# Spreading one much-gathered table row over 1024 copies, and moving a row norm's last step from VectorE to ScalarE, in a four-stage graph network kernel

## The reference, cut to what matters

```
net 0 (SAGE):  three layers  h = relu(h @ Ws + mean_over_edges(h[src]) @ Wn + b)
net 1 (GAT):   two attention layers with graph norms, then a mean over edges
net 2 (jumping knowledge), h = x, for i in 0..3:
    agg = segment_sum((h * norm_src)[src], dst) * norm_dst
    h = relu(agg @ Ws[i] + bs[i])
    h = relu(batchnorm(h) * gammas[i] + betas[i]);  xs.append(h)
  out = relu(max(xs) @ lin1_w + lin1_b)
net 3 (GCN):   three layers
```

## Time and profile before

| what | value |
|---|---|
| median of 3 runs | 6672.85 us (6664.08 to 6673.42) |
| the profiled execution, its own time | 6654.82 us |
| its span in the trace | 6653.0 us |
| mean granted TensorE clock | 0.814 |
| busy: PE, DVE, POOL, ACT | 71%, 68%, 61%, 46% of the span |
| DMA | 1292.14 MB, mean 194 GB/s |

### The profile page before, as it was taken

One profiled execution on the slowest core, in us unless ns is written; L12 is line 12 of the kernel. 1 busy time (PEld: TensorE's weight loads), 2 busy tenths in 40 slices (PEclk: granted clock), 3 DMA queues, 4 the chain that ended last, 5 costly groups with the idle time before them and its releaser, 6 DMA issues. The chain is left out here.

```text
span 6653.0 us, 86619 instructions
## 1 busy us (share of the span) xinstructions
PE 4751.0 (71%) x23528; PEld 3218.9 (48%) x23532; DVE 4503.1 (68%) x13695; ACT 3061.7 (46%) x6979; POOL 4040.8 (61%) x3991
## 2 busy tenths in 40 slices
PE   6999998989988724796335455545999996598221
PEld 4667776645568403694223233312666664465111
DVE  4788887333369827888885566776888885654554
ACT  3566665643334104454444444434888873364000
POOL 5566664754445477667667676675333335674777
PEclk9999998989999755795557766766999998799555
DMA  6999886987778424795445697855777776675232
GB/s 160 244 270 278 252 253 202 296 241 244 239 230 265 127 53 105 236 348 162 127 134 148 130 138 133 141 96 144 269 271 276 275 255 185 205 212 165 87 91 82
DMA packets 1104141, 1292.14 MB, mean 194 GB/s; under 512 B 133903, under 2 KB 815679, under 8 KB 1097390
## 3 DMA queue, kind: packets, MB, share of 16 engines
q1 hardware_dynamic: 973518, 1032.63, 49.1%
q0 software_dynamic: 130144, 253.97, 18.9%
HBM read 607.93 MB, written 682.10 MB: 194 GB/s over the span
## 5 line engine op out<-in xcount | busy, mean ns | idle before, releaser
L570 POOL DMA_INDIRECT jk_layer_msg<-jk,idx_jk x588 | 592.9, 1008 | 255.1 <-issue 175.3
L1057 PE MATMUL jk_layer_sum_ps<-ident,jk_layer_weighted 128*128 128x128 f32 x784 | 182.3, 375 | 540.3 <-ACT jk_layer_weighted L1023 540.3
L2084 POOL TENSOR_TENSOR rows_moved<-rows_x_in,w_lonely_row 128x512 f32<-128x512 f32 x98 | 152.3, 1554 | 563.0 <-DVE rows_x L671 537.0
L1057 PEld LDWEIGHTS jk_layer_sum_ps<-ident,jk_layer_weighted 128*128 128x128 f32 x784 | 116.4, 185 | 655.7 <-ACT jk_layer_weighted L1023 655.7
L696 PE MATMUL sage_nodes_h_ps<-sage_nodes_h_t,w_ws 128*128 128x512 f32 x784 | 353.7, 594 | 0.0
L1198 DVE COPY sage_h<-sage_turn 128x512 f32<-128x512 f32 x98 | 67.8, 692 | 421.0 <-PE sage_turn L687 421.0
L2283 PE MATMUL gcn_end_sum_ps<-ident,gcn_end_rows 128*128 128x128 f32 x196 | 54.7, 435 | 394.5 <-DVE gcn_end_rows L2276 394.5
L894 ACT ACTIVATE sage_nodes_h_t<-sage_nodes_h_ps,w_b_c 128x512 f32<-128x512 f32 x392 | 248.2, 684 | 172.6 <-PE sage_nodes_h_ps L696 172.2
L570 POOL DMA_INDIRECT sage_msg<-h,idx x196 | 185.8, 948 | 230.6 <-ACT sage_weighted L1023 151.6
L696 PE MATMUL jk_layer_h_ps<-jk_layer_sum_t,w_jk_w 128*128 128x512 f32 x392 | 315.0, 900 | 0.2
L1079 DVE TENSOR_TENSOR_SCAN jk_layer_sum_t<-goes_on,jk_layer_sum_t,jk_layer_sum_ps 128x512 f32<-128x512 uint8 x196 | 249.8, 1274 | 92.7 <-PE jk_layer_sum_ps L1057 92.7
(11 more groups left out here) (454 smaller groups left out, 16050.7 us busy)
## 6 DMA issues: line engine op xcount, KB each, us to landing
h<-sage_nodes_h SPq DMA_DIRECT2D x196, 512.0 KB
h_t<-sage_h_t SPq DMA_DIRECT2D x98, 512.0 KB, 4.9
h<-sage_h SPq DMA_DIRECT2D x98, 512.0 KB
jk_t<-jk_layer_h_t SPq DMA_DIRECT2D x196, 256.0 KB
rows_layers<-jk_t SPq DMA_DIRECT2D x49, 1024.0 KB, 6.0
r<-rows_h SPq DMA_DIRECT2D x98, 512.0 KB, 7.3
second_x_in<-u SPq DMA_DIRECT2D x147, 260.0 KB
jk<-jk_layer_h SPq DMA_DIRECT2D x147, 256.0 KB
```

Source lines behind the costliest of these rows:

```text
L570: pool.indirect_dma_start(out=into[:, g.number % depth, s, :], out_offset=None, in_=table, in_offset=bass.IndirectOffsetOnAxis(ap=index_ti ...
L1057: mm = pe.transpose(ps[:, c, at_s], self.weighted[:, g.b, s, c * P:(c + 1) * P], self.K.ident[:])
L2084: pool.tensor_tensor(moved[:, g.b], x_in[:, g.number % 3], to_subs(W.lonely_row), ALU.add).then_inc(lonely_added.sem, 1)
```

## The change

It has two parts that don't touch each other.

First, the row shared by lonely sources gets 1024 copies in each of jk0, jk1 and jk2 (rows SLOTS to SLOTS + 1023), and `K.idx_jk` of an edge with a lonely source is SLOTS plus the low ten bits of its place. The copies are made in `fetch_block` (class `LonelyRows`: DVE makes three diagonal matrices, PE spreads each over all partitions with one matmul, DVE copies them to SBUF, SP stores 512 KB to each of the three tables), and `jk_start_block` loses its row, its transpose, its copy and its stores.

Second, in `sage_end_block` the step z = (y - mean) / root moves from DVE (four tensor_scalar) to ACT (four activations with `Identity`, scale 1/root and bias -mean/root). DVE keeps the reciprocal, and makes the bias with one small scalar_tensor_tensor (`invert`, now first in DVE's list, ahead of `carry`). The ACT stage stands first in ACT's list, and the stages behind it (turn_x1, copy_x1, make_u, out_u, out_att, store_u) get one more step of lag.

```
+LONELY_ROWS = 1024
+class LonelyRows:
+    def vector_diag(self, dve):
+        dve.tensor_scalar(W.jk_const[:], W.jk_b[:], 0.0, None, ALU.max).then_inc(self.const_made, 1)
+        dve.wait_ge(self.const_made, 1)
+        for i in range(LAYERS - 1):
+            ins = dve.tensor_scalar(self.diag[:, i, :], self.K.ident[:], W.jk_const[:, i:i + 1], None, ALU.mult)
+        ins.then_inc(self.diag_made, 1)
+    def tensor_spread(self, pe):
+        pe.wait_ge(self.diag_made, 1)
+        for i in range(LAYERS - 1):
+            mm = pe.matmul(self.ps[:, i, :], self.K.ones[:], self.diag[:, i, :], start=True, stop=True)
+        mm.then_inc(self.spread, 1)
+    def vector_keep(self, dve):
+        dve.wait_ge(self.spread, 1)
+        dve.tensor_copy(self.rows[:], self.ps[:]).then_inc(self.kept, 1)
+    def sync_store(self, sp):
+        sp.wait_ge(self.kept, 1)
+        for i in range(LAYERS - 1):
+            copies = self.tables[f"jk{i}"][SLOTS:SLOTS + LONELY_ROWS].rearrange("(p r) d -> p r d", p=P)
+            sp.dma_start(copies, self.rows[:, i:i + 1, :].broadcast_to([P, LONELY_ROWS // P, D])).then_inc(self.stored, 16)
...
 fetch_block:
     def _(sp):
+        lonely.sync_store(sp)
         counts.sync_store(sp)
+        lonely.sync_wait(sp)
     def _(pe):
+        lonely.tensor_spread(pe)
         for t in range(ET):
             counts.tensor_count(pe, t)
     def _(dve):
+        lonely.vector_diag(dve)
+        lonely.vector_keep(dve)
         for t in range(ET):
             counts.vector_hot(dve, t)
...
 places_block:
-        dve.tensor_scalar(K.idx_jk[:], where[:], float(SLOTS), None, ALU.min)
+        link(dve.tensor_single_scalar(low_i[:], K.place[:], LONELY_ROWS - 1, op=ALU.bitwise_and))
+        link(dve.tensor_copy(low[:], low_i[:]))
+        link(dve.scalar_tensor_tensor(low[:], where[:], float(SLOTS), low[:], ALU.is_ge, ALU.mult))
+        dve.scalar_tensor_tensor(K.idx_jk[:], where[:], float(SLOTS), low[:], ALU.min, ALU.add)
...
 sage_end_block:
-        run_groups(sp, EG, [(load_own, 0), (load_x, 0), (store_x1, 3), (store_u, 4)])
+        run_groups(sp, EG, [(load_own, 0), (load_x, 0), (store_x1, 3), (store_u, 5)])
-        run_groups(pe, EG, [(tensor_sum, 0), (make_u, 3), (make, 1), (turn_x1, 2)])
+        run_groups(pe, EG, [(tensor_sum, 0), (make_u, 4), (make, 1), (turn_x1, 3)])
-        run_groups(act, EG, [(out_u, 3), (scalar_weigh, -1), (copy_x1, 2), (scalar_root, 1)])
+        def apply(g):
+            wait_for(act, shift_made, g)
+            wait_for(act, x1_turned, g.lag(2))
+            wait_for(act, z_stored, g.lag(2))
+            for s in range(SUB):
+                ins = act.activation(z[:, g.b, s, :], y[:, g.b, s, :], ACT.Identity, bias=less_mean[:, g.b, s, :], scale=norm.root[:, g.b, s, :])
+            ins.then_inc(norm.done.sem, 1)
+        run_groups(act, EG, [(apply, 2), (out_u, 4), (scalar_weigh, -1), (copy_x1, 3), (scalar_root, 1)])
-        def apply(g):
-            wait_for(dve, x1_turned, g.lag(2))
-            wait_for(dve, z_stored, g.lag(2))
-            norm.vector_apply(dve, g, y, z)
+        def invert(g):
+            wait_for(dve, norm.has_root, g)
+            dve.reciprocal(norm.root[:, g.b, :, 0], norm.root[:, g.b, :, 0]).then_inc(norm.has_inverse.sem, 1)
+            wait_for(dve, norm.has_inverse, g)
+            wait_for(dve, norm.done, g.lag(2))
+            dve.scalar_tensor_tensor(less_mean[:, g.b, :, 0], norm.moments[:, g.b, :, 0], -1.0, norm.root[:, g.b, :, 0],
+                                     ALU.mult, ALU.mult).then_inc(shift_made.sem, 1)
-        run_groups(dve, EG, [(carry, 0), (out_att, 3), (apply, 2), (add, 1)])
+        run_groups(dve, EG, [(invert, 2), (carry, 0), (out_att, 4), (add, 1)])
...
 jk_start_block: jk_const, its transpose on PE, the copy on DVE and the three stores of one row each are removed
```

More of the change, by code:

```diff
@@ L561, in pool_wait, with __init__, sync_wait @@
         pool.wait_ge(self.arrived, 16 * (self.end - self.first))
+class LonelyRows:
+    def __init__(self, nc, ph, K, W, tables):
+        self.nc, self.K, self.W, self.tables = nc, K, W, tables
+        n = LAYERS - 1
+        self.diag, self.rows, self.ps = ph.sb("const_diag", [P, n, P]), ph.sb("const_rows", [P, n, D]), ph.ps("const_ps", [P, n, D])
+        self.const_made, self.diag_made, self.spread, self.kept, self.stored = (
+            ph.sem(f"const_{k}") for k in ("made", "diag_made", "spread", "kept", "stored"))
+    def vector_diag(self, dve):
+        W = self.W
+        dve.tensor_scalar(W.jk_const[:], W.jk_b[:], 0.0, None, ALU.max).then_inc(self.const_made, 1)
[16 more added lines that the diff above has]
+            sp.dma_start(copies, self.rows[:, i:i + 1, :].broadcast_to([P, LONELY_ROWS // P, D])).then_inc(self.stored, 16)
+    def sync_wait(self, sp):
+        sp.wait_ge(self.stored, 16 * (LAYERS - 1))
 def pool_gather(pool, g, index_tile, used, table, into, arrived):
@@ L571, in pool_gather, with fetch_block @@
                                 in_offset=bass.IndirectOffsetOnAxis(ap=index_tile[:, cols(g, SUB, s, 1)], axis=0)).then_inc(arrived.of(g), 16)
-def fetch_block(nc, name, K, table, kept, counts_table):
+def fetch_block(nc, name, K, W, tables, kept):
     ph = Phase(nc, name, 0)
+    table = tables["u"][0:V_ROWS]
     arrived = [ph.sem(f"arrived{b}") for b in range(4)]
-    counts = SourceCounts(ph, K, counts_table)
+    counts = SourceCounts(ph, K, tables["counts"])
+    lonely = LonelyRows(nc, ph, K, W, tables)
     block = ph.block()
@@ L1264, in make_u @@
             layer_rows(pe, u_ps[:, :, 0:D + 4], [(W.wide["gat1"], x1_t[:, g.b])]).then_inc(u_made.sem, 1)
[L1265 removed]
+        run_groups(pe, EG, [(lambda g: sums.tensor_sum(pe, g), 0), (make_u, 4), (make, 1), (turn_x1, 3)])
     @block.scalar
@@ L1280, in out_u @@
             ins.then_inc(u_out.sem, 1)
-        run_groups(act, EG, [(out_u, 3), (lambda g: sums.scalar_weigh(act, g), -1), (copy_x1, 2), (lambda g: norm.scalar_root(act, g, W.eps), 1)])
+        def apply(g):
[5 more added lines that the diff above has]
+            ins.then_inc(norm.done.sem, 1)
+        run_groups(act, EG, [(apply, 2), (out_u, 4), (lambda g: sums.scalar_weigh(act, g), -1), (copy_x1, 3), (lambda g: norm.scalar_root(act, g, W.eps), 1)])
     @block.vector
@@ L1305, in out_att @@
             dve.tensor_tensor(u[:, g.b, :, 0:D], u[:, g.b, :, 0:D], to_subs(W.row["gat1_b"]), ALU.add).then_inc(u_biased.sem, 1)
-        run_groups(dve, EG, [(lambda g: sums.vector_carry(dve, g, [made]), 0), (out_att, 3), (apply, 2), (add, 1)])
+        run_groups(dve, EG, [(invert, 2), (lambda g: sums.vector_carry(dve, g, [made]), 0), (out_att, 4), (add, 1)])
     ph.close()
@@ L1805, in _ @@
         link(dve.tensor_tensor(K.l2_weight[:], K.l2_weight[:], K.norm_dst[:], ALU.mult))
[L1807 to L1817, removed]
     ph.close()
@@ L2516, in resnorm_gnn @@
             scores = kept[:, :, D:D + 2]
-            fetch_block(nc, "fetch", K, tables["u"][0:V_ROWS], kept, tables["counts"])
+            fetch_block(nc, "fetch", K, W, tables, kept)
             softmax_block(nc, "softmax1", K, scores, 2, tables["counts"], 0, 42)
```

13 lines of the change are left out of this document (5 added, 8 removed).

## The result

The changed kernel takes 6607.54 us (median of 4 runs, 6602.84 to 6622.04) where the kernel before takes 6673.14 us beside it (6664.08 to 6678.98, 4 runs): ratio 0.9907, 95% interval 0.9887 to 0.9926, 65.6 us less. The forecast of 34.8 us less had the sign right and was too small. Its profiled execution is the longest of its four, 6622.04 us (span 6619.9).

What follows compares the result with a forecast made beforehand. POOL's gather issue plus tails was taken to set the jk layers, DVE to bound the last SAGE layer. Savings of 19.5 (copies), 0.3 (jk_start_block) and 15 (norm), 34.8 us, off the median 6672.85 gave 6638; range 6616 to 6663.

Steps and rivals of the forecast that it cites:

- The copies: Jk layers: spread reads shorten layer 1 by 11.7, layer 2 by 7.8 and layer 3 by 0 us; sum 19.5.
- The share: Jk layers 1 and 2: gather packets would hold 25 to 40% of the DMA engines, against 57.0% before in layer 1.
- the borders: Ends of jk layers 1 and 2: POOL's idle tails of 27.88 and 27.20 us would fall to 19.4.
- The failed step: fetch_block: some 3 us of added DVE and PE work ahead of the counting, hidden by POOL's 196 gathers, costs nothing.
- The stores: fetch_block: three 512 KB stores of copies on SP's queue priced at 0, with 3 us of loss as far bound.
- The norm on ACT: Last SAGE layer: group period falls from 6.96 to 6.62 us over 46 groups, saving 15 us after 0.7 back.
- The wait for the root: Last SAGE layer: DVE's reciprocal, no longer covered by the scan, waits 0.43 us for ACT's root in each group.
- Rival (d): Last SAGE layer: ACT's list becomes the loop, period 7.7 us, kernel 14 us slower at 6687; chance 0.04.
- The base: Whole kernel: the saving taken off the runs' median 6672.85, as the profiled execution was 18 us shorter than that median.
- the forecast's lower end of 6616: Whole kernel: 6629 at both upper bounds (23 + 21 us saved), lowered for the 9 us by which three earlier runs differ.

Runs made afterwards that it cites:

- e6: Changed kernel with sage_end_block as before and the indices using only 16 of the 1024 copies; 6624.08 us, jk layers 1 to 3 836.0 us.
- e12: Kernel before plus the diagonals, matmuls and PSUM copy ahead of the counting in fetch_block, without stores; 6619.62 us, fetch block 255.8 us.
- e2: Changed kernel with sage_end_block as before, so only the copies; 6623.09 us, ratio 0.9968 to the kernel before, fetch block 255.3 us.
- e9: Changed kernel with the scan (carry) ahead of invert in DVE's list; 6690.49 us, ratio 1.0076 to the kernel before, last SAGE layer 437.0 us.
- e17: Changed kernel with carry ahead of invert on DVE and out_u and weigh ahead of apply on ACT; 6586.20 us, ratio 0.9900 to the kernel before.
- e14: Kernel before, with the counting in fetch_block made to wait for two PE matmuls; 6659.36 us, fetch block 265.3 us.
- e13: Kernel before, with the counting in fetch_block made to wait for one PE matmul; 6635.53 us, fetch block 255.3 us.
- e15: Kernel before, with the counting in fetch_block made to wait for three PE matmuls; 6655.05 us, fetch block 256.8 us.

## Why the prediction was wrong

**The copies** were right in mechanism and size: 19.5 forecast, 19.0 between means of ten executions each. By layer it is 11.6 for layer 1 (11.7 forecast), 8.9 for layer 2 (7.8), and layer 3 is 1.5 longer. The share fell to 26 to 28% (25 to 40 forecast), the borders to 18.2 and 18.7 us (19.4 forecast), and layer 3 gave nothing, its length 282.6 before and 282.8 after in the two profiles. That the copies must only be spread over few rows was left open and is answered by e6.

**The failed step** is the price of the work ahead of the counting in `fetch_block`: "since POOL's 196 gathers last longer than the counting; so nothing". That the work is hidden from the path is true: the path is POOL's issue. But it moved the start of the counting, and so its position against the gathers, and the path itself became 9 to 10 us shorter. I looked only for what the new work could add to POOL, and the only bound I gave for the block beside 0 was 3 us of loss, from the stores. The stores, which I priced at 0 beside it, do cost nothing: 255.8 us without them (e12), 255.3 with them (e2). A sign of it was there to be read: in the kernel before, a gather's median in this block is 0.974 us, against 0.947 in the jk layers, and in the timeline the gathers beside the counting take 1.04 to 1.05 one after the other. POOL's own instruction was being stretched by DVE, and whatever shifts DVE's start could change that. That a shift of some 3 us fell on the faster side was luck.

**The norm on ACT** was right in mechanism and 3 us too small. The wait for the root measured 0.36 us for 0.43, and from aggregation to scan 1.07 for 1.18; so DVE's own loop is 6.96 - 1.24 + 0.77 = 6.49 and the measured period 6.51, not 6.60. ACT's four activations took 1.65 us, within the 1.64 to 1.75 forecast (0.095 us for each second pointer instead of 0.12), and PE, whose loop was forecast at 6.6, kept up with 6.51 at 92% busy. 46 groups at 0.45 are 20.7; of that 18.0 reached the block's length, so the longer start and end cost 2.7 and not 0.7. Rival (d) needed ACT's list to become the loop. It didn't in this order, and e9 shows how near a loop through ACT lay: one pair exchanged on DVE, and it costs 86 us.

**The base.** I took the profiled execution's distance of 18 us to the median as a level that the changed kernel would share. It isn't one: after's median lies 14 us below its own profiled execution. With the terms as measured (46 us) the forecast would have been 6627, still 19 above the measured median of that series. That part isn't explained by any block. The measured median lies below the forecast's lower end of 6616 because both came together: the terms as measured give 6627, and the 19 us without them 6619. (That end was also mis-summed: 6629 less the 9 us named is 6620.) Against the mean of the four comparisons, 52.8 us, the blocks leave 7 us open.

## What to carry to other kernels

Work that is hidden behind another engine's longer row isn't free of effect where the two engines run in step: if the path engine's instruction shows two durations (here 0.94 and 1.05 us) in one loop, each many times over, ask what meets it, and price a shift of the start both ways. Where a gather's packets take over twice as long as elsewhere at the same bytes, count how many indices name one row; sixteen copies were as good as 1024. When a step moves to another engine, follow in that engine's list what stands behind it and who of its releasers waits for that in the same step: the same four activations cost 86 us behind the wrong neighbour (e9) and gave a further 8 to 12 us behind the right one (e17).

## What the runs showed of the hardware

- Many reads of one 512 B row by indirect gathers hold the DMA engines 53 to 61% of a layer where rows are stored beside them (layers 1 and 2, ten executions) and 38 to 42% where none are (layer 3); reads spread over 16 or 1024 rows hold them 24 to 28% in all three, for the same 6272 packets and 12.86 MB. Issue is slowed little, by 4 us of 258 in layer 1 and by none in layer 2; the messages land late.
- A burst of back-to-back f32 multiplications on VectorE stretched a gather's issue on GpSimd from 0.94 us to 1.65 and 2.74 us, to 0.11 and 0.13 us after the burst's end.
- With PE at half clock (granted 0.50), short bf16 comparisons on VectorE and gathers on GpSimd fall into one of two steady patterns, of 1.35 or 1.25 us, by an offset of 0.4 us at the start, and stay in it for the whole counting (before and e14; e2 and e13). Both patterns occur at 0.50, so the clock doesn't decide between them. With PE at full clock (1.00 in e15 and in the profile after) they don't lock: a pair of tiles is counted about every 1.06 us, and most gathers keep 0.94.
